# The first attention of a two-layer kernel: values stationary, the aggregate turned, norms from a product

## The chip, the cores and the metric

One Trainium2 chip (trn2), one core of it. The metric is the device time of one execution in microseconds (us), as the median of several runs. PE is TensorE (matrix products), DVE is VectorE, ACT is ScalarE, POOL is GpSimd, SP issues DMAs. All matrix products here are in float32 unless said otherwise; a float32 product shows as two MATMUL and two LDWEIGHTS records in the trace, a float32 transpose as one of each.

## The reference, cut to what matters

There are 4096 tokens in 16 sequences of 256, with 128 features. Four blocks follow each other: a recurrent mixer, a mixture of 32 small experts, the first attention, and a second attention with a mixture of 8 experts. The change touches the first attention alone:

```python
q, g = split(tokens @ Wqg)      # 16 heads, keys of 16, values and gates of 64
k, v = split(tokens @ Wkv)
q, k, v = l2norm(q), l2norm(k), l2norm(v)
attn = square(relu(q @ k.T))
aggr = attn @ v                 # per head: 256 x 64
n = norm(aggr, axis=-1)
out = tanh(n) * aggr / max(n, 1e-12) * tanh(silu(g))
y = out.reshape(tokens, 16 * 64) @ Wout
```

## The kernel before

The program has phases, one for each block; the first attention is the third, between two points at which all engines meet. Its work is one sequence at a time (256 queries and keys, in two tiles of 128), as a pipeline of four stages over the sequences: `fetch` (gather the expert outputs, form the input and normalise it), `front` (queries, keys, values, gates and their norms), `att` (scores, relu, square, aggregate) and `tail` (the last two aggregates, norms, gate, output product). `pipeline` calls each engine's `half(fetch, front, att, tail)` once for each step, with the sequences that stand one behind the other in the four stages; 19 steps in all, of which ten run in a loop of two steps a turn. Inside a step every engine goes through g = 0 to 7, the eight pairs of heads, and its program is written out by hand: what stands ahead of what on an engine is the order of the lines of `half`, and engines meet at semaphores alone. So a waiting instruction holds up all that stands behind it on its engine.

For each pair g PE makes the scores with keys on partitions (`scores`, L1091), ACT applies relu into one of four `attn` buffers (L831), DVE squares it (L1571), but POOL does for pairs 2, 3 and 6 (L601), and two pairs later PE adds up the aggregate (`aggregate`, L1103). There the squared scores are the stationary operand (128 columns) and the values the moving one (64 columns), so the aggregate has queries on partitions:

```python
mm = pe.matmul(psum[:, 4 + j, ...], attn[g % RING][:, h, ...128 queries], v[q.p][:, c, ...64], ...)
```

The aggregate of four pairs (half hf = 0 or 1) fills banks 4 and 5. Then the half's tail begins: ACT copies it out and squares it (`take_aggregate`, L843), DVE sums the squares over each head's 64 values (`norm_of`, L1573), POOL makes 1/length and length (`length_of`, L603: a power of -0.5, L608), ACT takes the tanh (L850), POOL scales the gate by tanh and 1/length (`scale_gate`, L612), DVE multiplies aggregate and gate (`gated_output`, L1578), PE turns the result (`turn_oT`, L1121), ACT and DVE copy one tile each out of PSUM (`take_oT`, L855 and L1583). When both halves are there, PE multiplies by Wout (L1168), DVE adds the residual (L1693) and SP stores it. The half 0 is worked on from g = 5 of stage `att` on, half 1 in stage `tail`.

Two PSUM banks (6 and 7, `ring`) serve all other products of the phase in turn; `fill` (L1083) waits for the last reader of a bank before it is written again. On DVE the inverse roots of the norms of queries, keys and values (`inverse_root`, twelve small instructions, L1550 to L1561) stand at g = 3 and give POOL the factor by which it scales the values (L648). `normalise3` (L1607) makes the next sequence's normalised input with the factor `rstd3` of POOL (L655); PE turns it (L1184), ACT copies it out as x3T (L904), and the next step's products start from it.

## Time and profile before

| what | us |
|---|---|
| median of 3 runs | 2004.08 |
| lowest, highest | 1994.43, 2009.70 |
| span of the profiled execution | 2019.7 |
| of it, the phase of the first attention | about 385 to 1225 |

The profiled execution has no other time beside its span; the span is 15.6 us above the median of the three runs. Rows of the timeline have the start, the duration from the first start to the last end of a merged piece, engine, line, names, shapes and count; [..] at the end is the idle time of the engine ahead of the piece and what ended it. PEclk is the share of TensorE's 2.4 GHz that was granted: 1.00 or, at the lower of its two levels (1.2 GHz), 0.50.

### The profile page before, as it was taken

What the parts mean: (1) busy time and instruction counts of PE and PEld (TensorE: products, weight loads), DVE (VectorE), ACT (ScalarE), POOL (GpSimd) and SP (SyncE); (2) the same over time, 40 slices, a digit from 0 to 9 for tenths busy, and PEclk for the clock granted to TensorE, in tenths of its full rate; (3) what the DMA queues carried; (4) which work ended last, traced back from release to release, by engine and by line L of the source; (5) the groups of instructions that cost most, each with busy time, mean ns of one, the idle gap of its engine ahead of it and who ended that gap; (6) DMA issues with size and microseconds to landing.
All of it is one profiled execution on the core that took longest, in us unless ns stands there. A gap on an engine that the chain in (4) does not pass through costs nothing.

```text
span 2019.7 us, 28317 instructions
## 1 busy us (share of the span) xinstructions
PE 1449.9 (72%) x8634; PEld 933.4 (46%) x8635; DVE 1233.7 (61%) x2840; ACT 750.5 (37%) x1206; POOL 949.0 (47%) x1080
## 2 busy tenths in 40 slices
PE   3434326478787878778878872899989989984876
PEld 2222214146665656566666671334333333334765
DVE  6877841387876777778778742565746556553332
ACT  1101002144444444444444430445544454541221
POOL 2346476466665656566666442131312213124554
PEclk7555555578887878888888875777876687786777
DMA  4000006100000000000000003000000000001110
GB/s 123 22 24 14 12 7 127 43 5 7 8 8 1 6 6 6 6 6 6 6 6 9 3 3 94 6 9 17 14 10 8 16 8 16 5 11 37 43 42 12
DMA packets 73355, 40.91 MB, mean 20 GB/s; under 512 B 23811, under 2 KB 68716, under 8 KB 73284
## 3 DMA queue, kind: packets, MB, share of 16 engines
q1 hardware_dynamic: 50530, 24.02, 4.3%
q0 software_dynamic: 20384, 11.67, 2.9%
q10 hardware_dynamic: 2370, 4.35, 0.8%
q8 instruction: 36, 0.59, 0.1%
q14 instruction: 35, 0.29, 0.1%
HBM read 31.11 MB, written 23.87 MB: 27 GB/s over the span
## 4 chain that ended last, share of the span: by engine, by line
PE 45%; DVE 25%; issue 10%; POOL 8%; ACT 5%; another core or an unknown queue 3%; DMA 2%; ACTq 1%; POOLq 1%; SPq 0%; DVEq 0%
PE psum L1117 8%; PE psum L1221 6%; PE psum L1242 5%; PE psum L1168 4%; DVE o L1581 3%; PE psum L1251 3%; PE psum L1211 2%; PE psum L1154 2%; POOL yg L631 2%; POOL out L753 2%; PE psum L1126 2%; PE psum L1145 1%; PE psum L1283 1%; DVE rden L1433 1%
## 5 line engine op out<-in xcount | busy, mean ns | idle before, releaser
L1117 PE MATMUL psum<-v,attn 128*128 128x64 f32 x2048 | 293.2, 304 | 25.6 <-ACT aggr L846 17.1
L1117 PEld LDWEIGHTS psum<-v,attn 128*128 128x128 f32 x2048 | 277.2, 217 | 61.9 <-issue 45.7
L1741 DVE TENSOR_REDUCE terms<-psum 128x2 bf16<-128x512 f32 x256 | 170.2, 692 | 94.8 <-PE psum L1242 87.0
L683 POOL TENSOR_SCALAR veps<-meanvar 128x2 f32<-128x2 f32 x32 | 6.1, 192 | 423.4 <-DVE meanvar L1719 423.4
L921 ACT ACTIVATE prob<-psum 128x512 f32<-128x512 f32 x256 | 143.6, 597 | 100.8 <-PE psum L1211 98.6
L1221 PE MATMUL psum<-prob,v 128*32 128x256 f32 x1024 | 172.2, 466 | 0.8 <-ACT pvT L926 0.8
L631 POOL DMA_INDIRECT yg<-ye_dram,routel x128 | 142.1, 1110 | 59.8 <-issue 37.3
L560 POOL DMA_INDIRECT xe_dram<-rows_out,route x128 | 130.9, 1023 | 39.7 <-issue 39.4
L1242 PE MATMUL psum<-k_highT,q_highT 32*128 32x256 bf16 x512 | 127.7, 344 | 29.7 <-DVE terms L1741 27.0
L1126 PE MATMUL psum<-ident,o 128*128 128x128 f32 x256 | 50.1, 360 | 118.8 <-DVE silu_g L1675 82.1
L831 ACT ACTIVATE attn<-psum 128x1024 f32<-128x1024 f32 x128 | 130.1, 1017 | 14.0 <-PE psum L1100 11.2
L608 POOL TENSOR_TENSOR o_inv<-o_max,minus_half 128x16 f32<-128x16 f32 x32 | 100.2, 3133 | 2.7
L1126 PEld LDWEIGHTS psum<-ident,o 128*128 128x128 f32 x256 | 40.1, 187 | 132.5 <-DVE o L1581 57.6
L648 POOL TENSOR_TENSOR v<-v,inv 128x2048 f32<-128x2048 f32 x16 | 70.7, 4419 | 63.1 <-DVE inv L1561 63.1
L1571 DVE TENSOR_TENSOR attn<-attn 128x1024 f32<-128x1024 f32 x80 | 99.3, 1242 | 0.0
L1581 DVE TENSOR_TENSOR o<-aggr,gate 128x1024 f32<-128x1024 f32 x32 | 90.1, 2815 | 13.6 <-POOL gate L620 13.6
L601 POOL TENSOR_TENSOR attn<-attn 128x1024 f32<-128x1024 f32 x48 | 91.1, 1897 | 7.9 <-ACT attn L831 7.9
L606 POOL TENSOR_SCALAR o_max<-o_norm 128x16 f32<-128x16 f32 x32 | 11.2, 350 | 176.1 <-DVE o_norm L1576 174.4
L1221 PEld LDWEIGHTS psum<-prob,v 128*32 128x32 f32 x1024 | 58.6, 125 | 71.1 <-issue 44.3
L1168 PE MATMUL psum<-w_out,oT 128*128 128x128 f32 x512 | 88.5, 353 | 0.9 <-DVE oT L1585 0.9
L1211 PE MATMUL psum<-qT,kT 64*128 64x256 bf16 x512 | 87.8, 314 | 0.0
L1168 PEld LDWEIGHTS psum<-w_out,oT 128*128 128x128 f32 x512 | 87.0, 268 | 1.2 <-issue 1.2
(300 smaller groups left out, 3088.7 us busy)
## 6 DMA issues: line engine op xcount, KB each, us to landing
x4n_dram<-x4n SPq DMA_DIRECT2D x16, 256.0 KB, 2.2
w<-in_w POOLq DMA_DIRECT2D x48, 64.0 KB, 2.7
x_in<-in_x SPq DMA_DIRECT2D x8, 256.0 KB, 2.9
xe_dram<-zero_rows SPq DMA_DIRECT2D x8, 256.0 KB, 3.3
x_dram<-x1s SPq DMA_DIRECT2D x8, 256.0 KB
xe_dram<-rows_out,route POOLq DMA_INDIRECT x128
xe<-xe_dram SPq DMA_DIRECT2D x16, 128.0 KB
ye_dram<-ye SPq DMA_DIRECT2D x16, 128.0 KB, 2.2
```

The costliest lines, as they stand in the source:

```text
L560: pool.indirect_dma_start(xe_dram, bass.IndirectOffsetOnAxis(ap=where[:, j, K0 + k:K0 + k + 1], axis=0), rows_out[p][:, j, :], None, bound ...
L631: pool.indirect_dma_start(yg[fetch.p][:, j, k, :], None, ye_dram, bass.IndirectOffsetOnAxis(ap=where[:, j, K0 + k:K0 + k + 1], axis=0), bo ...
L831: act.activation(r[:], psum[:, 2 * (g % 2):2 * (g % 2) + 2, :], ACT.Relu).then_inc(s["relu_made"], 1)
L921: act.activation(prob[head % 4][:], bank[head % 3][:], ACT.Exp, scale=SCALE).then_inc(s["exp_made"], 1)
L1117: mm = pe.matmul(psum[:, 4 + j, (head % HALF) * DV:(head % HALF + 1) * DV], attn[g % RING][:, h, c * SEQ + j * P:c * SEQ + (j + 1) * P], v ...
L1126: mm = pe.transpose(b[:, c * P:(c + 1) * P], o[:, j, c * P:(c + 1) * P], ident[:])
L1168: mm = pe.matmul(b[:, j * D:(j + 1) * D], oT[:, j, c, :], w_out[:, c, :], start=(c == 0), stop=(c == PAIRS - 1))
L1211: mm = pe.matmul(bank[head % 3][:, c * SEQ:(c + 1) * SEQ], kT4[att.p][part, head // 2, c * P:(c + 1) * P], qT4[att.p][part, head // 2, :], ...
L1221: mm = pe.matmul(bank[3][part, t * SEQ:(t + 1) * SEQ], v4[q.p][:, c, head, :], prob[head % 4][:, c * SEQ:(c + 1) * SEQ], start=(c == 0), s ...
L1242: mm = pe.matmul(bank[4 + a2][:, b2 * SEQ:(b2 + 1) * SEQ], q_highT[part, 2 * jp + b2, j * P:(j + 1) * P], k_highT[part, :], start=True, st ...
L1581: dve.tensor_tensor(o[:], aggr[:], gate[q.p][:, :, 512 * hf:512 * hf + 512], ALU.mult).then_inc(s["o_made"], 1)
L1741: dve.tensor_reduce(terms4[:, 0, j, head:head + 2, 6, 0], bank[4 + a2].rearrange("q (b k) -> q b k", b=2), AX, ALU.max, negate=True).then_ ...
```

## The change

The aggregate product swaps its operands: the 64 value columns of a head are loaded as weights and 256 queries stream past, so that the aggregate has the 64 dimensions of a head on partitions, two heads above each other (the heads of a pair write partitions 0 to 63 and 64 to 127). There are four products of 256 columns for a pair where there were eight of 64. It is already turned, so `turn_oT` and both `take_oT` go. In exchange the gate, scaled by POOL as before, is turned on PE (`turn_gate`), and DVE multiplies it straight out of PSUM into `oT` (`gated_output`, two instructions of 128x512 for a half where there were one of 128x1024 and a copy of 128x512). The sum of squares over a head now runs over partitions: PE multiplies the squared aggregate, as weights, by a new constant of two columns, `head_of`, that selects the head (`sum_squares`, eight products for a half), and DVE copies the 16 norms out of PSUM (`norm_of`). `aggr` has two buffers. The places in the order change too, as the diff shows.

```diff
-        aggr = sb("aggr", [P, 2, 512])
-        aggr_sq = sb("aggr_sq", [P, 2, 512])
-        o = sb("o", [P, 2, 512])
+        aggr = two("aggr", [P, 4, SEQ])
+        aggr_sq = sb("aggr_sq", [P, 4, SEQ])
...
                 if att:
                     length_of(att, 0)
+                if att:
+                    square(att, POOL_PAIRS[2])
                 if fetch:
                     hold(s["var3"], fetch.n)
...
                     pool.tensor_tensor(rstd3[:], veps3[:], minus_half[:, 0:2], ALU.pow).then_inc(s["rstd3"], 1)
                 if att:
                     scale_gate(att, 0)
-                if att:
-                    square(att, POOL_PAIRS[2])
...
             def take_aggregate(q, hf):
-                wait(act, s["o_made"], 2 * (q.n - 1) + hf)
+                wait(act, s["oT_made"], 4 * (q.n - 2) + 2 * hf + 2)
                 act.wait_ge(s["attn_read"], PAIRS * (q.n - 1) + 4 * hf + 4)
-                act.activation(aggr[:], psum[:, 4:6, :], ACT.Copy).then_inc(s["aggr_out"], 1)
+                act.activation(aggr[hf][:].rearrange("q (b a) t -> q b (a t)", b=2), psum[:, 4:6, :], ACT.Copy).then_inc(s["aggr_out"], 1)
...
-                    if tail and g == 0:
-                        take_aggregate(tail, 1)
-                    if tail and g == 2:
+                    if tail and g == 3:
                         tanh_of_norm(tail, 1)
                     if front and g in (1, 2):
...
+                    if tail and g == 1:
+                        take_aggregate(tail, 1)
...
-                    if front and g == 5:
-                        gate_tanh(front, 1)
-                    if att and g == 6:
+                    if att and g == 7:
                         tanh_of_norm(att, 0)
...
+                    if front and g == 6:
+                        gate_tanh(front, 0)
+                        gate_tanh(front, 1)
...
-                for j in range(2):
+                at = 4 + g % 4 // 2
+                for c in range(2):
                     for h in range(2):
                         head = 2 * g + h
-                        for c in range(2):
-                            mm = pe.matmul(psum[:, 4 + j, (head % HALF) * DV:(head % HALF + 1) * DV], attn[g % RING][:, h, c * SEQ + j * P:c * SEQ + (j + 1) * P],
-                                           v[q.p][:, c, head * DV:(head + 1) * DV], start=(c == 0), stop=(c == 1))
+                        mm = pe.matmul(psum[DV * h:DV * h + DV, at, g % 2 * SEQ:(g % 2 + 1) * SEQ], v[q.p][:, c, head * DV:(head + 1) * DV],
+                                       attn[g % RING][:, h, c * SEQ:(c + 1) * SEQ], start=(c == 0), stop=(c == 1))
...
-            def turn_oT(q, hf):
+            def sum_squares(q, hf, x):
+
+                m = 2 * (q.n - 1) + hf + 1
+                b = fill(x, [(s["o_norm_made"], m)], [(s["aggr_sq_made"], m)])
                 for j in range(2):
-                    x = OT_BANK[hf][j]
-                    b = fill(x, [(s["oT_dve" if j else "oT_act"], 2 * (q.n - 1) + hf + 1)], [(s["o_made"], 2 * (q.n - 1) + hf + 1)])
+                    for a4 in range(4):
+                        at = HALF * j + 2 * a4
+                        mm = pe.matmul(b[:, at:at + 2], aggr_sq[:, a4, j * P:(j + 1) * P], head_of[:], start=True, stop=True)
+                mm.then_inc(s["norm_ps"], 1)
+
+            def turn_gate(q, hf):
+                for j in range(2):
+                    m = 4 * (q.n - 1) + 2 * hf + j + 1
+                    b = fill(OT_BANK[hf][j], [(s["oT_made"], m)], [(s["gated"], m)])
                     for c in range(4):
-                        mm = pe.transpose(b[:, c * P:(c + 1) * P], o[:, j, c * P:(c + 1) * P], ident[:])
-                    mm.then_inc(s["oT_ps"], 1)
+                        mm = pe.transpose(b[:, c * P:(c + 1) * P], gate[q.p][:, j, 512 * hf + c * P:512 * hf + (c + 1) * P], ident[:])
+                    mm.then_inc(s["gateT_ps"], 1)
...
                     if tail and g == 1:
-                        turn_oT(tail, 0)
+                        turn_gate(tail, 0)
+                    if tail and g == 2:
+                        sum_squares(tail, 1, 0)
                     if tail and g == 5:
-                        turn_oT(tail, 1)
+                        turn_gate(tail, 1)
...
+                    if att and g == 6:
+                        sum_squares(att, 0, 1)
                     if fetch and g == 7:
                         b = fill(0, [], [(s["xn3_made"], fetch.n)])
...
             def norm_of(q, hf):
                 wait(dve, s["o_len_made"], 2 * (q.n - 1) + hf)
-                dve.wait_ge(s["aggr_sq_made"], 2 * (q.n - 1) + hf + 1)
-                dve.tensor_reduce(o_norm[:], aggr_sq[:].rearrange("q j (h d) -> q (j h) d", d=DV), AX, ALU.add).then_inc(s["o_norm_made"], 1)
+                dve.wait_ge(s["norm_ps"], 2 * (q.n - 1) + hf + 1)
+                dve.tensor_copy(o_norm[:], ring[1 - hf][:, 0:2 * HALF]).then_inc(s["o_norm_made"], 1)
...
             def gated_output(q, hf):
-                wait(dve, s["oT_ps"], 4 * (q.n - 1) + 2 * hf)
-                dve.wait_ge(s["gated"], 4 * (q.n - 1) + 2 * hf + 2)
-                dve.tensor_tensor(o[:], aggr[:], gate[q.p][:, :, 512 * hf:512 * hf + 512], ALU.mult).then_inc(s["o_made"], 1)
...
+                wait(dve, s["y3_ps"], q.n - 1)
+                dve.wait_ge(s["aggr_out"], 2 * (q.n - 1) + hf + 1)
+                for j in range(2):
+                    dve.wait_ge(s["gateT_ps"], 4 * (q.n - 1) + 2 * hf + j + 1)
+                    dve.tensor_tensor(oT[:, j, 4 * hf:4 * hf + 4, :], ring[OT_BANK[hf][j]][:].rearrange("q (c t) -> q c t", c=4), aggr[hf][:, :, j * P:(j + 1) * P], ALU.mult).then_inc(s["oT_made"], 1)
...
                     if tail and g == 1:
+                        gated_output(tail, 0)
+                    if tail and g == 2:
                         norm_of(tail, 1)
-                    if tail and g == 1:
-                        take_oT(tail, 0)
...
-                    if tail and g == 4:
-                        gated_output(tail, 1)
...
                     if tail and g == 5:
-                        take_oT(tail, 1)
-                    if att and g == 5:
-                        norm_of(att, 0)
+                        gated_output(tail, 1)
...
+                    if att and g == 6:
+                        norm_of(att, 0)
                     if fetch and g == 6:
                         normalise3(fetch)
-                    if att and g == 7:
-                        gated_output(att, 0)
```

What is left out: the declaration and the DMA of `head_of` among the weights, the names of semaphores, and the removed `take_oT` on ACT and DVE.

The three places that matter for the prediction, as they stand in the built programs. First PE, the last part of a step (g = 6 and 7), before: w_out with oT is the output product, ident with terms turns queries and keys, qT with kT are scores, v with attn the aggregate, ident with xn turns the next sequence's input.

```order
L1168 MATMUL psum<-w_out,oT 128x128 [waits oT_dve,oT_act]
L1168 MATMUL psum<-w_out,oT 128x128 x15
L1179 MATMUL psum<-ident,terms 128x128 [waits terms_made,oT_dve]
...
L1179 MATMUL psum<-ident,terms 128x128 [waits x3_made]
...
L1100 MATMUL psum<-qT,kT 128x256 [waits relu_made]
...
L1117 MATMUL psum<-v,attn 128x64 [waits attn_made]
...
L1179 MATMUL psum<-ident,terms 128x128 [waits qkT_act]
...
L1179 MATMUL psum<-ident,terms 128x128 [waits qkT_dve]
...
L1184 MATMUL psum<-ident,xn 128x128 [waits xn3_made,qkT_act]
```

And PE after, same place:

```order
L1172 MATMUL psum<-w_out,oT 128x128 [waits oT_made]
L1172 MATMUL psum<-w_out,oT 128x128 x15
L1183 MATMUL psum<-ident,terms 128x128 [waits terms_made,oT_made]
...
L1183 MATMUL psum<-ident,terms 128x128 [waits x3_made]
...
L1120 MATMUL psum<-head_of,aggr_sq 128x2 [waits aggr_sq_made,qkT_dve]
L1120 MATMUL psum<-head_of,aggr_sq 128x2 x7
L1092 MATMUL psum<-qT,kT 128x256 [waits relu_made]
...
L1109 MATMUL psum<-attn,v 64x256 [waits attn_made]
...
L1183 MATMUL psum<-ident,terms 128x128 [waits qkT_act]
...
L1183 MATMUL psum<-ident,terms 128x128 [waits o_norm_made]
...
L1190 MATMUL psum<-ident,xn 128x128 [waits xn3_made,qkT_act]
```

Behind the first two turns of terms stands a new block, the products of `aggr_sq` with `head_of`, which wait for the DVE copy of kT; the last turn before x3T now waits for the norms.

Second POOL, from the scaling of the values (v with inv) to the end of a step, before:

```order
L648 TENSOR_TENSOR v<-v,inv 128x2048 [waits v_copied]
...
L606 TENSOR_SCALAR o_max<-o_norm 128x16 [waits o_norm_made]
L608 TENSOR_TENSOR o_inv<-o_max,minus_half 128x16 [waits pool_chain]
L610 TENSOR_TENSOR o_len<-o_norm,o_inv 128x16 [waits pool_chain]
...
L653 TENSOR_SCALAR veps<-meanvar 128x2 [waits var3]
L655 TENSOR_TENSOR rstd<-veps,minus_half 128x2 [waits pool_chain]
...
L616 TENSOR_TENSOR o_factor<-o_tanh,o_inv 128x16 [waits gate_made,o_tanh_made]
L620 TENSOR_TENSOR gate<-gate,o_factor 128x512 [waits o_factor_made]
L620 TENSOR_TENSOR gate<-gate,o_factor 128x512
...
L601 TENSOR_TENSOR attn<-attn 128x1024 [waits relu_made]
```

After:

```order
L648 TENSOR_TENSOR v<-v,inv 128x2048 [waits v_copied]
...
L606 TENSOR_SCALAR o_max<-o_norm 128x16 [waits o_norm_made]
L608 TENSOR_TENSOR o_inv<-o_max,minus_half 128x16 [waits pool_chain]
L610 TENSOR_TENSOR o_len<-o_norm,o_inv 128x16 [waits pool_chain]
...
L601 TENSOR_TENSOR attn<-attn 128x1024 [waits relu_made]
...
L655 TENSOR_SCALAR veps<-meanvar 128x2 [waits var3]
L657 TENSOR_TENSOR rstd<-veps,minus_half 128x2 [waits pool_chain]
...
L616 TENSOR_TENSOR o_factor<-o_tanh,o_inv 128x16 [waits gate_made,o_tanh_made]
L620 TENSOR_TENSOR gate<-gate,o_factor 128x512 [waits o_factor_made]
L620 TENSOR_TENSOR gate<-gate,o_factor 128x512
```

The square of pair 6 (attn from attn) has moved from the end to between the lengths and rstd; the lengths still wait for o_norm.

Third DVE, g = 4 to 6, before: silu_g is the gate, attn the square, terms the split of queries and keys, x from yg the combination of expert outputs, xn the normalised input.

```order
L1581 TENSOR_TENSOR o<-aggr,gate 128x1024 [waits gated]
...
L1675 SCALAR_TENSOR_TENSOR silu_g<-tanh_g,psum 128x512 [waits g_tanh,gate_made] x2
...
L1571 TENSOR_TENSOR attn<-attn 128x1024 [waits relu_made]
L1626 TENSOR_TENSOR terms<-qk,terms 128x64x16 [waits high_made]
...
L1585 COPY oT<-psum 128x512 [waits dve_chain,oT_ps]
L1576 TENSOR_REDUCE o_norm<-aggr_sq 128x16 [waits aggr_sq_made,o_len_made]
...
L1594 SCALAR_TENSOR_TENSOR x<-yg,routel,x1l 128x128 [waits yg_landed1]
...
L1571 TENSOR_TENSOR attn<-attn 128x1024 [waits relu_made]
...
L1693 TENSOR_TENSOR x<-x_kept,psum 128x256 [waits y3_ps,x3_stored0]
L1697 COPY kT<-psum 128x1024 [waits terms_ps]
L1610 TENSOR_SCALAR xn<-x,meanvar,rstd 128x128 [waits rstd3,var3]
L1611 TENSOR_SCALAR xn<-x,meanvar,rstd 128x128
```

After:

```order
L1677 SCALAR_TENSOR_TENSOR silu_g<-tanh_g,psum 128x512 [waits g_tanh,gate_made] x2
...
L1577 TENSOR_TENSOR attn<-attn 128x1024 [waits relu_made]
L1630 TENSOR_TENSOR terms<-qk,terms 128x64x16 [waits high_made]
...
L1589 TENSOR_TENSOR oT<-psum,aggr 128x512 [waits gateT_ps]
...
L1589 TENSOR_TENSOR oT<-psum,aggr 128x512 [waits gateT_ps]
...
L1598 SCALAR_TENSOR_TENSOR x<-yg,routel,x1l 128x128 [waits yg_landed1]
...
L1577 TENSOR_TENSOR attn<-attn 128x1024 [waits relu_made]
...
L1693 TENSOR_TENSOR x<-x_kept,psum 128x256 [waits y3_ps,x3_stored0]
L1697 COPY kT<-psum 128x1024 [waits terms_ps]
L1582 COPY o_norm<-psum 128x16 [waits norm_ps,o_len_made]
L1614 TENSOR_SCALAR xn<-x,meanvar,rstd 128x128 [waits rstd3,var3]
L1615 TENSOR_SCALAR xn<-x,meanvar,rstd 128x128
```

The product of aggregate and gate has gone from ahead of the gate's silu to behind the split; o_norm, before a sum ahead of the combination of expert outputs, is now a copy that stands behind the first kT and directly ahead of xn.

## Rows read from the trace of the kernel before

**Rows 1.** The page: its first line
```profile
span 2019.7 us, 28317 instructions
```

**Rows 2.** Windows by stage: the columns, the first phases, the first attention
```profile
core 0: us, PE busy (x) PEld busy (x) DVE busy (x) ACT busy (x) POOL busy (x), PEclk, DMA share, GB/s
0.00:385.00 385.00, 144.07 (x608) 93.83 (x609) 225.67 (x666) 48.41 (x125) 191.98 (x239) 0.56 0.21 48
385.00:1225.00 840.00, 664.66 (x4192) 504.96 (x4192) 614.67 (x982) 390.56 (x512) 507.95 (x408) 0.82 0.03 6
```

**Rows 3.** Timeline of DVE: the sum x3 of sequence 1, then of 14
```profile
501.49 0.42 DVE L1693 TENSOR_TENSOR x<-x_kept,psum 128x256 f32<-128x256 f32 x1 [2.55 <-PE psum L1168]
...
1157.72 0.42 DVE L1693 TENSOR_TENSOR x<-x_kept,psum 128x256 f32<-128x256 f32 x1 [5.15 <-PE psum L1168]
```

**Rows 4.** Timeline of PE, one sequence: start, duration, idle time before
```profile
748.04 1.97 PE L1126 MATMUL psum<-ident,o 128*128 128x128 f32 x8 [4.94 <-DVE silu_g L1675]
...
751.78 3.67 PE L1117 MATMUL psum<-v,attn 128*128 128x64 f32 x16 [1.23 <-ACT aggr L846]
755.24 5.72 PE L1168 MATMUL psum<-w_out,oT 128*128 128x128 f32 x32
760.80 1.37 PE L1179 MATMUL psum<-ident,terms 128*128 128x128 f16 x16
...
766.06 0.43 PE L1184 MATMUL psum<-ident,xn 128*128 128x128 f32 x2 [0.74 <-ACT qT L900]
...
772.91 1.94 PE L1154 MATMUL psum<-w_v,x3T 128*128 128x512 f32 x4
776.03 1.09 PE L1126 MATMUL psum<-ident,o 128*128 128x128 f32 x8 [1.19 <-issue]
```

**Rows 5.** Timeline of DVE, same sequence
```profile
742.68 4.64 DVE L1581 TENSOR_TENSOR o<-aggr,gate 128x1024 f32<-128x1024 f32 x1
...
748.43 1.21 DVE L1571 TENSOR_TENSOR attn<-attn 128x1024 f32<-128x1024 f32 x1
749.57 1.21 DVE L1626 TENSOR_TENSOR terms<-qk,terms 128x1024 f16<-128x1024 f32 x1
...
776.02 1.21 DVE L1576 TENSOR_REDUCE o_norm<-aggr_sq 128x16 f32<-128x1024 f32 x1
...
785.14 1.46 DVE L1675 SCALAR_TENSOR_TENSOR silu_g<-tanh_g,psum 128x512 f32<-128x512 f32 x2 [1.17 <-ACT tanh_g L880]
786.52 0.69 DVE L1550 TENSOR_SCALAR norm<-norm 128x96 f32<-128x96 f32 x1
...
791.50 4.64 DVE L1581 TENSOR_TENSOR o<-aggr,gate 128x1024 f32<-128x1024 f32 x1
```

**Rows 6.** Timeline of POOL, same sequence
```profile
758.90 0.69 POOL L655 TENSOR_TENSOR rstd<-veps,minus_half 128x2 f32<-128x2 f32 x1
...
777.77 2.94 POOL L608 TENSOR_TENSOR o_inv<-o_max,minus_half 128x16 f32<-128x16 f32 x1
...
785.25 1.89 POOL L601 TENSOR_TENSOR attn<-attn 128x1024 f32<-128x1024 f32 x1
790.67 4.39 POOL L648 TENSOR_TENSOR v<-v,inv 128x2048 f32<-128x2048 f32 x1 [3.53 <-DVE inv L1561]
```

**Rows 7.** Timeline of ACT: the turned input x3T leaves PSUM
```profile
766.53 0.39 ACT L904 ACTIVATE x3T<-psum 128x256 f32<-128x256 f32 x1 [0.60 <-PE psum L1184]
```

**Rows 8.** Timeline of PE in the first phase: products of 64 weight columns
```profile
51.21 1.98 PE L1034 MATMUL psum<-x2T,sw 128*64 128x256 f32 x8
53.11 1.92 PE L1030 MATMUL psum<-gate_w,x2T 128*128 128x32 f32 x8
```

**Rows 9.** Windows: after PE's idle time, and later (columns as in rows 2)
```profile
748.00:759.00 11.00, 9.72 (x46) 8.93 (x47) 9.75 (x21) 5.59 (x7) 4.41 (x5) 0.50 0.00 0
759.00:791.00 32.00, 29.64 (x216) 21.30 (x215) 22.59 (x39) 17.92 (x24) 23.35 (x22) 1.00 0.04 9
```

**Rows 10.** Waits, 450 to 1150 us: what POOL waited for longest
```profile
POOL o_max L606 <- DVE o_norm L1576: 134.7, 21, 13.7
```

More of the change, by code:

```diff
@@ L194, in build_program @@
         head_mask = sb("head_mask", [P, 4])
+        head_of = sb("head_of", [P, 2])
         token_start = sb("token_start", [P, 2])
@@ L443, in _ @@
                              (b_o[:], a["b_o"].partition_broadcast(P)), (gate1_w[:], a["gate1_w"]),
-                             (gate1_b[:], a["gate1_b"].partition_broadcast(P)), (norms[:], a["norms"]), (head_mask[:], a["head_mask"]),
+                             (gate1_b[:], a["gate1_b"].partition_broadcast(P)), (norms[:], a["norms"]), (head_mask[:], a["head_mask"]), (head_of[:], a["head_of"]),
                              (token_start[:], a["token_start"]), (steps_of[:], a["steps_of"].partition_broadcast(P)),
@@ L838, in gate_tanh @@
             def gate_tanh(front, j):
-                wait(act, s["o_made"], 2 * (front.n - 2))
+                wait(act, s["gateT_ps"], 4 * (front.n - 2))
                 act.wait_ge(s["silu_made"], 4 * (front.n - 1) + 2 * j + 2)
@@ L1134, in half @@
                 elif tail:
-                    readers[0] = readers[1] = []
+                    readers[0], readers[1] = [], [(s["o_norm_made"], 2 * tail.n - 1)]
                 if front:
@@ L1660, in half @@
                     if tail and g == 1:
+                        gated_output(tail, 0)
+                    if tail and g == 2:
                         norm_of(tail, 1)
-                    if tail and g == 1:
-                        take_oT(tail, 0)
                     if front and g == 3:
@@ L1951, in lay_out @@
         "head_mask": (np.arange(P)[:, None] // DH % 4 == np.arange(4)[None, :]).astype(np.float32),
+        "head_of": (np.arange(P)[:, None] // DV == np.arange(2)[None, :]).astype(np.float32),
         "token_start": (np.arange(P)[:, None] + P * np.arange(2)[None, :]).astype(np.float32),
```

21 lines of the change are left out of this document (6 added, 15 removed).

## The prediction

> **What bounds the kernel now.** I read the page first, for the span [rows 1], then windows by stage. The first attention takes 840 us, and in them PE is busy 665, DVE 615, POOL 508 and ACT 391 [rows 2]: no engine is full, so the length comes from who waits for whom. The period next: the residual sum of sequence 1 starts at 501.49 and that of sequence 14 at 1157.72 [rows 3], so 13 steps take 656.2 us, 50.5 each. Some of them hold the turn of the loop and are longer; the step that I follow has none and takes 791.50 - 742.68 = 48.8 us from one product o to the next [rows 5]. Then the timelines, engine by engine, of that step. The reader is to see four things in them.
>
> 1. PE idles once for long: 4.94 us ahead of the turn at 748.04, until DVE has read a bank (silu_g) [rows 4]. DVE reads it late because o, ahead of it in its order, takes 4.64 us [rows 5].
> 2. o is slow because POOL scales the values meanwhile: 4.39 us at 790.67, and DVE's o at 791.50 ends (796.14) when POOL is through (795.06) and 1.2 us more have gone [rows 5, 6]. The small TENSOR_SCALAR at 786.52 takes 0.69 where it ends just behind POOL's square at 785.25; silu_g at 785.14, with one operand in PSUM, takes 1.46 for two beside the same square [rows 5, 6]. So a DVE instruction with all operands in SBUF can wait for POOL's to end, and one that reads PSUM does not.
> 3. Behind PE's long idle time the clock is down: 0.50 in 748 to 759, then 1.00 until 791 [rows 9]. The aggregate of a pair takes 3.67 at the lower clock [rows 4].
> 4. POOL waits 134.7 us in 21 times for o_norm [rows 10]; the norms of half 0 are still early enough: POOL has rstd by 758.90 + 0.69 = 759.6, while PE turns the next input only at 766.06 [rows 4, 6]. 6.5 us of slack, which the change spends.
>
> **What gets cheaper.** The aggregate of a pair: eight MATMUL records with 64 weight columns and 256 moving ones. The first phase has just that shape: x8 start at 51.21, and the next piece at 53.11, so 1.90 us, in a stage whose granted clock is 0.56 on average, so mostly 1.2 GHz [rows 2, 8]. The old aggregate takes 3.67 less an overlap of 0.2 at the lower clock, 3.47 [rows 4]. So the new one is 0.55 of it at the lower clock; at the higher one half of 1.90, 0.95, against 1.8. Some 0.85 x 8 = 6.8 us of PE a sequence. DVE loses o (4.64 and 1.2), two sums of 1.21 (one at 776.02 [rows 5]) and two copies of oT (some 0.65 each), 9.5 us, and gets four products out of PSUM of 0.65 and two small copies, 3 us. ACT loses two copies.
>
> **What gets dearer.** `sum_squares`: 16 weight loads of 128 columns for a half. The nearest row is the old aggregate itself, also 16 loads of 128 columns: 3.5 us at 1.2 GHz and 1.8 at 2.4 [rows 4], twice a sequence. PE is left with 6.8 - 3.6 = 3.2 us less. One DMA more for head_of lies among the weights, beside the first phases: nothing.
>
> The Trainium skill (TensorEngine Tiling (Array Packing), Key Properties) says that a change of tiling mode drains the array, which speaks against products of 64 columns between those of 128. The change of shape between 51.21 and 53.11 shows no gap [rows 8], and the row prevails: 0 us.
>
> **The path.** What decides is where the norms are now made. The chain that closes on itself in each step, with the time from x3T being ready (ACT, 766.53 + 0.39 = 766.92 [rows 7]):
>
> Front, to the norms of half 1. Before they are there at 776.02 + 1.21 = 777.24 [rows 5], 10.3 us behind x3T. Now: scores 0.3, w_qk 1.9 (as w_v at 772.91 [rows 4]), two aggregates 1.9, scores 0.3, w_v 1.8, the wait for DVE's copy 1.1 (from 774.85 to 776.03 [rows 4]), turn 1.0, scores 0.3, the wait for ACT's copy 0.4 and one aggregate 1.0, w_v 1.8, such a wait again 1.1, sum_squares 1.8, copy 0.3: 15.0 us.
>
> Middle, to w_out. Unchanged in kind: POOL's lengths, square, gate, square, from 777.24 to 785.25 + 1.89 = 787.14, 9.9 us [rows 5, 6]. Of them the lengths are 3.5 (the power 2.94 and two small ones). ACT's tanh of the gate stands behind the tanh of these lengths, so silu_g comes 2.2 us behind the lengths, and the inverse roots behind it meet POOL's gate and square, which run without a gap. With all operands in SBUF they wait, as at 786.52 [rows 5], and end 3.5 us behind the square (787.14 to 790.67 [rows 6]). Then POOL scales the values, 4.4, and now DVE's square of pair 4 is what waits for it, plus its own 1.2. Split 2.1, two products 1.3. In all 9.9 + 3.5 + 4.4 + 1.2 + 2.1 + 1.3 = 22.4 us. The saved o is thus given back: the block falls on the next instruction with SBUF operands.
>
> The Trainium skill states the rule behind it (SBUF — State Buffer, Who interferes with whom): a DVE instruction with two SBUF inputs contends with a GpSimd instruction that reads SBUF, and the second one blocks. The rows agree (4.64 against 1.2); were it not so the chain would be the 3.4 us shorter by which the short case below is shorter.
>
> End, from w_out to x3T. Before 766.92 - 755.24 = 11.7 us [rows 4, 7], since the norms of half 0 were made beside w_out. Now they stand behind it on PE: w_out 5.5 (as at 755.24, where half of it runs at the lower clock), the turns of terms 0.9, DVE's copy of kT 0.7, sum_squares 1.8, copy 0.3, POOL's lengths 3.5, then the square of pair 6 1.9, which was moved ahead of rstd, rstd 1.0 [rows 6], and xn, turn and copy out 3.2. The two xn cost 0.35 each, but POOL goes on with its gate and blocks the second; bounds 2.5 and 3.9. In all 18.8. Meanwhile PE has only scores, an aggregate and two turns, 2.2 us, and idles for some 6.
>
> That idle time is longer than the 4.94 behind which the clock stood at 0.50 for 11 us [rows 4, 9], so the next front begins at 1.2 GHz: its first 8 us of work can cost 4 more. Part of it lies under waits for DVE; I take 2.0, with 0 and 4.2 as bounds.
>
> Sum: 15.0 + 2.0 + 22.4 + 18.8 = 58.2 us a step against 48.8, so 9.4 more. This holds for the 13 steps between sequence 1 and 14 [rows 3]. In the last two steps nothing is fetched: no x3T waits; there the cheaper aggregates, which ran at the lower clock, give back what POOL's chain costs, and the first step with `att` has the new end once: together 0. So 13 x 9.4 = 122 us. The profiled execution would go from 2019.7 to 2142; from the median of the runs, 2004.1, the same step gives 2126.
>
> **The bounds.** Short: PE at 2.4 GHz throughout (w_out 3.7), the inverse roots run through beside POOL's square (3.4 less), xn at 2.5: 15.0 + 19.0 + 16.3 = 50.3 us, 1.5 more a step, 2024 us. Long: the lower clock in the front (4.2) and again from w_out to the norms (7.4, 1.9, 0.7 and 3.6 where 5.5, 0.9, 0.7 and 1.8 stand), xn at 3.9: 19.2 + 22.4 + 24.2 = 65.8, 17.0 more, 2225 us.
>
> **Rivals.**
> A, the other sign: PE was the bound and the norms come in time. For it: PE's one long idle time hung on o, and without it 4.9 us of waiting and the slow stretch behind it (an aggregate at 3.5 for 1.8, w_out 1.8 dearer, a turn 0.9) would go, 9 us, and PE's 3.2. If the new end cost only its PE work, a step would be near 42 to 44 us: 13 x 5.5 = 70 less, 1934 us. It decides at w_out: the new end is at least 16.3 us long where 11.7 were, so w_out would have to start 4.6 us earlier than now (37.1 behind x3T), and the middle alone, with the norms of half 1 later by 4.7, forbids that. Chance 0.07.
> B, the short case: the chain as I say, but unblocked and at the higher clock; 50 to 54 us a step, 2020 to 2070. For it: DVE is relieved of 6.5 us. Against: the block needs no coincidence, POOL follows its own order. Chance 0.17.
> C, the long case, over 62 us a step: the gaps ahead of the aggregates of pairs 2, 3 and 4 (2 to 4 us each) keep the clock down in the middle too. Over 2175. Chance 0.14.
> D, the change does not do what it says: products of 64 columns stream no faster than those of 128, 1.8 us a pair. Then the front is 2.6 us longer, a step 61, 2160. The rows of the first phase speak against it [rows 8]. Chance 0.04.
>
> My forecast, 54 to 62 us a step, has 0.58. Its own range is 2072 to 2176, and 2040 to 2190 leaves out 2 in 10. A measurement here tells about 1% (20 us) from no change. Faster by more than that is A, 0.06; within it lie the rest of A and the bottom of B, 0.07; slower is the rest, 0.87.
>
> **What would show it.** Right: o_norm of half 0 is made 7 us or more behind the start of w_out; PE waits for xn 5 us or more in each step, at the turn of the next input; POOL's lengths of half 1 start 14 to 19 us behind x3T where it was 10.3; the square of pair 4 takes 2.5 us or more, and the first inverse root over 2; products out of PSUM 0.65 each; an aggregate 0.95 at the higher clock; granted clock of the phase below what it is now. Wrong, if the residual sums come less than 50 us apart, if x3T waits for ACT's qT instead of xn, or if the aggregates still take 1.8 us.

## The result and the profile after

| | before | after |
|---|---|---|
| median of 4 runs each, us | 1999.26 (1969.48 to 2009.70) | 2132.9 (2126.89 to 2139.55) |
| after over before | | 1.0734, 95% interval 1.0623 to 1.0845 |
| span of the profiled execution, us | 2019.7 | 2131.2 |

The changed kernel is 7.3% slower. A ratio leaves out disturbed executions and the medians don't: for the run all_moves below only 3 of the 17 executions of before count (1965.6 to 1984.0 us), which is why its median lies under that of before and its ratio above 1. The page of after, its first line:

```profile
span 2131.2 us, 27346 instructions
```

The windows view of the first attention's phase, about 960 us long now (columns as in [rows 2]):

```profile
385.00:1345.00 960.00, 670.54 (x3678) 388.66 (x3677) 574.45 (x978) 376.95 (x479) 493.82 (x407) 0.77 0.02 5
```

PE has 514 MATMUL records fewer than in [rows 2] and is busy 6 us longer: what the smaller work saves, the lower granted clock (0.77 for 0.82) takes back. DVE is relieved of 40 us. Both are idle for longer, so the time went into waits. The residual sums of sequences 1 and 14, on DVE:

```profile
503.06 0.42 DVE L1693 TENSOR_TENSOR x<-x_kept,psum 128x256 f32<-128x256 f32 x1 [2.16 <-PE psum L1172]
...
1270.72 0.42 DVE L1693 TENSOR_TENSOR x<-x_kept,psum 128x256 f32<-128x256 f32 x1 [5.86 <-PE psum L1172]
```

13 steps take 767.7 us, 59.05 each, where [rows 3] gave 50.48. 13 x 8.57 = 111.4 us, as much as the whole difference of the two spans (111.5). Where a step's time goes, by engine, first PE's timeline from one turn of the next input (L1190) to the next:

```profile
751.10 0.69 PE L1190 MATMUL psum<-ident,xn 128*128 128x128 f32 x2 [6.15 <-DVE xn L1615]
...
752.36 3.07 PE L1147 MATMUL psum<-w_qk,x3T 128*128 128x512 f32 x4
755.36 1.08 PE L1109 MATMUL psum<-attn,v 128*64 128x256 f32 x8
756.38 0.39 PE L1092 MATMUL psum<-qT,kT 64*128 64x256 f16 x4
...
766.73 2.20 PE L1120 MATMUL psum<-head_of,aggr_sq 128*128 128x2 f32 x16 [1.19 <-DVE v L1659]
...
769.40 1.97 PE L1109 MATMUL psum<-attn,v 128*64 128x256 f32 x8
...
784.04 1.96 PE L1128 MATMUL psum<-ident,gate 128*128 128x128 f32 x8 [3.79 <-DVE silu_g L1677]
...
791.62 5.69 PE L1172 MATMUL psum<-w_out,oT 128*128 128x128 f32 x32 [1.72 <-DVE oT L1589]
...
799.30 1.95 PE L1120 MATMUL psum<-head_of,aggr_sq 128*128 128x2 f32 x16 [0.78 <-DVE kT L1697]
...
809.73 0.69 PE L1190 MATMUL psum<-ident,xn 128*128 128x128 f32 x2 [5.27 <-DVE xn L1615]
```

PE now idles 5 to 6 us ahead of L1190, a wait that was not there, and still 3.8 us ahead of the turned gate. An aggregate takes 1.02 us from its start to the next product's at the higher clock (755.36 to 756.38) and 1.91 at the lower (769.40 to w_g at 771.31). ACT's timeline has the copy x3T from which I count a step:

```profile
751.83 0.38 ACT L896 ACTIVATE x3T<-psum 128x256 f32<-128x256 f32 x1 [3.95 <-PE psum L1190]
...
810.46 0.38 ACT L896 ACTIVATE x3T<-psum 128x256 f32<-128x256 f32 x1 [3.96 <-PE psum L1190]
```

DVE's timeline of the same step:

```profile
769.04 0.17 DVE L1582 COPY o_norm<-psum 128x16 f32<-128x16 f32 x1 [2.44 <-PE psum L1120]
...
777.36 1.82 DVE L1558 TENSOR_SCALAR guess<-norm 128x96 uint32<-128x96 uint32 x1
779.21 0.21 DVE L1560 TENSOR_SCALAR inv<-guess 128x96 uint32<-128x96 uint32 x1
...
784.43 3.45 DVE L1577 TENSOR_TENSOR attn<-attn 128x1024 f32<-128x1024 f32 x1
...
790.18 1.29 DVE L1589 TENSOR_TENSOR oT<-psum,aggr 128x512 f32<-128x512 f32 x2 [0.31 <-DVE terms L1634]
...
801.35 0.17 DVE L1582 COPY o_norm<-psum 128x16 f32<-128x16 f32 x1 [2.11 <-PE psum L1120]
808.30 0.34 DVE L1614 TENSOR_SCALAR xn<-x,meanvar,rstd 128x128 f32<-128x128 f32 x1 [6.77 <-POOL rstd L657]
```

and POOL's:

```profile
769.42 0.26 POOL L606 TENSOR_SCALAR o_max<-o_norm 128x16 f32<-128x16 f32 x1 [6.06 <-DVE o_norm L1582]
...
777.22 1.89 POOL L601 TENSOR_TENSOR attn<-attn 128x1024 f32<-128x1024 f32 x1
782.39 4.40 POOL L648 TENSOR_TENSOR v<-v,inv 128x2048 f32<-128x2048 f32 x1 [3.29 <-DVE inv L1567]
801.72 0.25 POOL L606 TENSOR_SCALAR o_max<-o_norm 128x16 f32<-128x16 f32 x1 [14.93 <-DVE o_norm L1582]
...
805.25 1.89 POOL L601 TENSOR_TENSOR attn<-attn 128x1024 f32<-128x1024 f32 x1
...
807.50 0.69 POOL L657 TENSOR_TENSOR rstd<-veps,minus_half 128x2 f32<-128x2 f32 x1
```

Read from 801.35 on: the norms of half 0 are copied 4 us behind the end of w_out; POOL waits 14.93 us for them and has the lengths 3.7 us after the copy, then needs 1.9 for the square that was moved ahead and 1.0 for rstd; only then DVE can normalise, and PE turn, the next input. The waits of 450 to 1250 add this up (POOL's was 134.7 in [rows 10]):

```profile
POOL o_max L606 <- DVE o_norm L1582: 295.0, 27, 18.1
...
DVE xn L1614 <- POOL rstd L657: 94.9, 14, 6.8
PE psum L1190 <- DVE xn L1615: 79.6, 14, 6.2
```

The granted clock in this step, by windows:

```profile
750.00:760.00 10.00, 8.59 (x34) 3.38 (x34) 7.37 (x10) 4.00 (x6) 8.31 (x8) 0.77 0.01 1
...
769.00:772.00 3.00, 3.00 (x13) 1.27 (x10) 1.36 (x3) 1.02 (x1) 2.50 (x2) 0.50 0.00 0
...
785.00:791.00 6.00, 3.52 (x17) 1.50 (x15) 5.66 (x7) 2.46 (x3) 1.79 (x1) 0.50 0.00 0
...
801.00:809.00 8.00, 3.46 (x31) 2.38 (x30) 0.88 (x3) 2.15 (x3) 6.77 (x8) 0.59 0.00 0
```

It is down behind each of PE's long waits: when w_qk starts (3.07 us, where w_v, of the same shape, takes 1.98 at 2.4 GHz), and from the turned gate into w_out. It also falls at 769, behind sum_squares of half 1, with no idle time of PE over 1.2 us since 752; w_g there takes 3.78 us for 1.98.

### The profile page after: what moved, and what is told of

It reads as the page before. It is cut to its first block, busy times and chain, and to the rows that moved or that the text cites. A ratio compares the mean times of both kernels' runs of the same rounds, so it can differ in the third digit from the quotient of the medians.

```text
span 2131.2 us, 27346 instructions
## 1 busy us (share of the span) xinstructions
PE 1448.7 (68%) x8122; PEld 815.6 (38%) x8123; DVE 1194.9 (56%) x2840; ACT 736.0 (35%) x1174; POOL 936.2 (44%) x1080
## 4 chain that ended last, share of the span: by engine, by line
PE 40%; DVE 30%; issue 12%; POOL 11%; ACT 3%; DMA 2%; another core or an unknown queue 1%; ACTq 1%; POOLq 1%; DVEq 0%; SPq 0%
PE psum L1227 6%; PE psum L1172 4%; PE psum L1248 4%; POOL o_inv L608 4%; PE psum L1120 3%; PE psum L1109 3%; DVE attn L1577 3%; PE psum L1257 3%; PE psum L1147 3%; PE psum L1217 2%; POOL out L753 2%; POOL got L744 2%; DVE silu_g L1677 2%; DVE v L1659 1%; PE psum L1289 1%
## 5 line engine op out<-in xcount | busy, mean ns | idle before, releaser
L1109 PE MATMUL psum<-attn,v 128*64 128x256 f32 x1024 | 169.9, 462 | 60.4 <-POOL attn L601 30.7
L631 POOL DMA_INDIRECT yg<-ye_dram,routel x128 | 146.7, 1146 | 41.4 <-issue 37.0
L1577 DVE TENSOR_TENSOR attn<-attn 128x1024 f32<-128x1024 f32 x80 | 134.7, 1683 | 9.3 <-ACT attn L831 9.3
L1109 PEld LDWEIGHTS psum<-attn,v 128*64 128x64 f32 x1024 | 72.8, 158 | 136.4 <-issue 62.5
L1172 PE MATMUL psum<-w_out,oT 128*128 128x128 f32 x512 | 95.4, 372 | 23.7 <-DVE oT L1589 23.7
L1172 PEld LDWEIGHTS psum<-w_out,oT 128*128 128x128 f32 x512 | 92.6, 284 | 35.8 <-DVE oT L1589 35.4
L1128 PE MATMUL psum<-ident,gate 128*128 128x128 f32 x256 | 48.6, 351 | 70.7 <-DVE silu_g L1677 48.2
L608 POOL TENSOR_TENSOR o_inv<-o_max,minus_half 128x16 f32<-128x16 f32 x32 | 93.8, 2933 | 2.7
L1120 PE MATMUL psum<-head_of,aggr_sq 128*128 128x2 f32 x512 | 65.7, 259 | 33.0 <-DVE v L1659 16.4
L889 ACT ACTIVATE qT<-psum 128x1024 f16<-128x1024 f16 x32 | 32.5, 1016 | 158.2 <-PE psum L1183 158.1
L1227 PEld LDWEIGHTS psum<-prob,v 128*32 128x32 f32 x1024 | 58.2, 125 | 69.0 <-issue 39.8
```

Of the source, the lines that this page charges most:

```text
L608: n = chain.step(pool.tensor_tensor(o_inv[:], o_max[:], minus_half[:], ALU.pow))
L631: pool.indirect_dma_start(yg[fetch.p][:, j, k, :], None, ye_dram, bass.IndirectOffsetOnAxis(ap=where[:, j, K0 + k:K0 + k + 1], axis=0), bo ...
L1109: mm = pe.matmul(psum[DV * h:DV * h + DV, at, g % 2 * SEQ:(g % 2 + 1) * SEQ], v[q.p][:, c, head * DV:(head + 1) * DV], attn[g % RING][:, h ...
L1172: mm = pe.matmul(b[:, j * D:(j + 1) * D], oT[:, j, c, :], w_out[:, c, :], start=(c == 0), stop=(c == PAIRS - 1))
L1227: mm = pe.matmul(bank[3][part, t * SEQ:(t + 1) * SEQ], v4[q.p][:, c, head, :], prob[head % 4][:, c * SEQ:(c + 1) * SEQ], start=(c == 0), s ...
L1577: dve.tensor_tensor(r[:], r[:], r[:], ALU.mult).then_inc(s["attn_made"], 1)
```

## The experiments

**The theories.** The expectations name them so. T1: the chain of the prediction sets the step (front, POOL's lengths, the blocked square, w_out, norms of half 0, POOL, rstd, xn), and most of the loss is the place of the norms of half 0 and POOL's order behind them. T2, the rival: PE's own work at the lower clock sets it, and the waits only move about. All kernels but b_norm_late are edits of the changed one. "Step" is the mean of 13 as above, from one profiled execution of each kernel. Most medians are of 2 executions, those of the last three rows of 10 to 12; an empty bracket means the same before as in the row above.

| run | median us (before beside it) | ratio, 95% interval | step us |
|---|---|---|---|
| after | 2132.9 (1999.26) | 1.0734 (1.0623 to 1.0845) | 59.05 |
| rstd_first | 2107.94 (2007.89) | 1.0503 (1.0342 to 1.0664) | 56.99 |
| sq6_back | 2142.45 | 1.0675 (1.0514 to 1.0836) | 58.69 |
| norm_before_wout | 2056.22 | 1.0246 (1.0075 to 1.0416) | 54.34 |
| norm1_early | 2095.72 | 1.0442 (1.0280 to 1.0605) | 56.39 |
| b_norm_late | 2155.98 (2015.76) | 1.0721 (1.0600 to 1.0842) | 60.14 |
| small_v | 2079.81 | 1.0342 (1.0254 to 1.0430) | 55.93 |
| half_aggr | 2118.92 | 1.0537 (1.0439 to 1.0634) | 58.02 |
| rstd_tanh | 2052.36 (2004.55) | 1.0252 (1.0158 to 1.0346) | 52.85 |
| v_late | 2118.04 | 1.0580 (1.0484 to 1.0677) | 57.96 |
| both_norms | 2022.40 (2015.76) | 1.0020 (0.9962 to 1.0077) | 51.98 |
| all_moves | 1995.60 (2004.55) | 1.0068 (0.9996 to 1.0140) | 49.88 |
| norm_mid | 2000.31 (2004.47) | 1.0006 (0.9959 to 1.0052) | 50.73 |

**norm_before_wout**: the norms of half 0 ahead of w_out on PE and ahead of combine on DVE.

```diff
+                    if att and g == 6:
+                        sum_squares(att, 0, 1)
                     if tail and g == 6:
...
-                    if att and g == 6:
-                        sum_squares(att, 0, 1)
```

> The changed kernel with sum_squares of half 0 ahead of the output product on PE, and its copy on DVE ahead of the combination of expert outputs. Theory 1: w_out starts 2 to 3 us later, but POOL works beside it and x3T follows w_out by 13 us instead of 19; a step of 52 to 54, 2045 to 2075 us. Theory 2: PE's work is the same, 2133.

It went nearly so (54.3 us a step, the time inside the range): 4.7 us a step and half the loss, by order alone, with the same instructions.

**b_norm_late**, the other way round: the kernel before, with nothing but the norms of half 0 put where the change has them.

```diff
-                    if att and g == 5:
-                        norm_of(att, 0)
...
+                    if att and g == 6:
+                        norm_of(att, 0)
                     if fetch and g == 6:
                         normalise3(fetch)
```

> The kernel BEFORE with one line moved: DVE's sum for the norms of half 0 stands behind the first kT, directly ahead of xn, where the changed kernel has its copy. Nothing of the swap. Theory 1 (the place of the norms costs): the slack of 6.5 us is spent, x3T comes 4 us later, PE idles there for 4 us or more and starts the front at the lower clock; a step of 53 to 56 instead of 48.8, 2055 to 2095 us against 2000. Theory 2 (the swap and its products cost): as before, 2000.

Slower than expected by 60 us: this one move costs the old kernel as much as the whole change costs (1.0721 against 1.0734). A part of what I had left out stands in its timelines of PE and ACT:

```profile
884.64 1.89 PE L1179 MATMUL psum<-ident,terms 128*128 128x128 f16 x16 [4.63 <-ACT qT L900]
...
883.46 0.22 ACT L853 ACTIVATE o_tanh<-o_len 128x16 f32<-128x16 f32 x1 [12.34 <-POOL o_len L610]
883.58 1.00 ACT L900 ACTIVATE qT<-psum 128x1024 f16<-128x1024 f16 x1
```

ACT's tanh of the lengths waits 12.34 us, and ACT's copy qT, which frees a PSUM bank for PE, is queued behind it. The change moves the tanh from g = 6 to g = 7 and so avoids the worst of this. The other part is a wait in the front that the chain doesn't have. ACT's copy of the aggregate of half 1, first in before, then in this run:

```profile
616.43 1.02 ACT L846 ACTIVATE aggr<-psum 128x1024 f32<-128x1024 f32 x1 [6.82 <-remote]
...
835.71 1.02 ACT L846 ACTIVATE aggr<-psum 128x1024 f32<-128x1024 f32 x1 [4.97 <-remote]
```

The trace names no releaser, DVE stands still beside ACT, and both go on 2 to 4 us behind the end that the trace gives PE's aggregate. Before has this wait in three of its 13 steps, which are its three long ones, this run in nine, after in none; where it comes from is open. So the run shows that late norms cost without the swap too, but not how much of the 7% they are; for the changed kernel norm_before_wout tells that.

**norm1_early**: the norms of half 1 ahead of the value products of g = 2, on PE and on DVE.

> The changed kernel with sum_squares of half 1 ahead of the second pair of value products instead of behind it, and the copy on DVE likewise. Theory 1: the norms of half 1 come 13.4 us behind x3T instead of 17.0, and all of the middle with them; a step of 55, 2086 us. Theory 2: 2133.

The norms of half 1 come 13.8 and 15.0 us behind x3T, where in after they come 17.0 and 18.0, and the step loses 2.7 us: near what was expected. It is the other cost of where the norms stand.

**rstd_first**: POOL makes rstd ahead of the lengths and of the square of pair 6.

```diff
-                if att:
-                    length_of(att, 0)
-                if att:
-                    square(att, POOL_PAIRS[2])
                 if fetch:
                     hold(s["var3"], fetch.n)
...
+                if att:
+                    length_of(att, 0)
+                if att:
+                    square(att, POOL_PAIRS[2])
```

> The changed kernel with one thing moved: POOL makes rstd of the next sequence ahead of the lengths of half 0. Theory 1 (the step closes through the norms: sum_squares, POOL's lengths and square, rstd, xn, x3T): x3T comes some 6.5 us earlier, PE's wait of 5 to 6 us for xn falls under 1.5, and the clock holds in the front; a step of 50 to 52 us instead of 58.6, 2035 us in all (2020 to 2060). Theory 2 (the extra products of PE and their clock make it slower, the order on POOL does not matter): no change, 2133.

A miss: 57.0 for 50 to 52. POOL's rstd is early, as wanted, but x3T still comes 6.0 us behind the norms here, and up to 6.7 in other steps. Its timelines of PE and ACT:

```profile
858.48 0.43 PE L1190 MATMUL psum<-ident,xn 128*128 128x128 f32 x2 [1.65 <-ACT qT L889]
...
857.22 0.22 ACT L854 ACTIVATE o_tanh<-o_len 128x16 f32<-128x16 f32 x1 [2.74 <-POOL o_len L610]
857.34 1.01 ACT L889 ACTIVATE qT<-psum 128x1024 f16<-128x1024 f16 x1
```

PE waits no more for xn but for a bank that ACT's qT frees (1.65 us here, 3.3 in most steps), and qT is queued behind the tanh, which waits for POOL. So the same late norms reach PE over a second engine.

**rstd_tanh**: rstd_first, and ACT's tanh of half 0 behind its copy x3T.

> rstd_first with one more move: ACT's tanh of the lengths of half 0 stands behind the copies of qT and x3T instead of ahead of them. In rstd_first x3T came 6.0 us behind the norms of half 0 though rstd was long there; the theory is that qT waited behind that tanh, which waits for POOL's lengths. Then x3T comes 4.0 to 4.5 us behind the norms, PE's wait for qT goes from 1.65 us to under 0.8, a step 55.2 instead of 57.0, 2085 us. If another wait stood behind it (POOL's square ahead of DVE's, the clock), no change, 2108.

Better than expected by 33 us; the profile of PE and ACT shows both waits gone:

```profile
825.51 0.43 PE L1190 MATMUL psum<-ident,xn 128*128 128x128 f32 x2 [0.74 <-ACT qT L887]
...
826.51 1.96 PE L1147 MATMUL psum<-w_qk,x3T 128*128 128x512 f32 x4 [0.24 <-ACT x3T L894]
...
825.98 0.38 ACT L894 ACTIVATE x3T<-psum 128x256 f32<-128x256 f32 x1 [0.60 <-PE psum L1190]
```

x3T comes 3.7 and 4.6 us behind the norms in turn (9.3 in after), and a step is 6.2 us shorter than in after by two moves. PE has no long idle time there any more, and w_qk takes 1.96 instead of 3.07: the two waits had cost the clock too, which I had not counted and which explains about 1 us of the surplus.

**sq6_back**: POOL's square of pair 6 behind the gate again, where it stood before.

> The changed kernel with POOL's square of pair 6 back behind the scaling of the gate, as before the change. Theory 1: rstd is 1.9 us earlier, so is x3T; a step of 56.7, 2108 us. Theory 2: no change, 2133. A third way: the aggregate of pair 6 now waits for the square and takes the gain back, 2125 or more.

A miss: no gain. From the residual sum to the next x3T it is 1.9 us shorter (11.5 for 13.4), as the square is; but the norms of half 1 then come at 18.5 and 19.8 instead of 17.0 and 18.0. PE doesn't wait for POOL's square there (its first aggregate starts at 872.46, directly behind w_qk); w_qk runs at the lower clock throughout (3.76 us), and sum_squares waits 1.85 us for DVE's value copy, for 1.19 in after. What ties this to the place of the square is open. The move of the square is no net part of the loss.

**small_v**: POOL scales one of 64 value columns.

```diff
-                    pool.tensor_tensor(vv, vv, inv3[:, 4 * HEADS:].unsqueeze(2).to_broadcast([P, 2 * HEADS, DV]), ALU.mult).then_inc(s["v_made"], 1)
+                    pool.tensor_tensor(vv[:, :, 0:1], vv[:, :, 0:1], inv3[:, 4 * HEADS:].unsqueeze(2).to_broadcast([P, 2 * HEADS, 1]), ALU.mult).then_inc(s["v_made"], 1)
```

> The changed kernel with POOL's scaling of the values cut to one of 64 columns a head; the other 63 stay unscaled, which the output has then too. Theory 1: DVE's square of pair 4 no longer waits (1.2 us instead of 3.45), so w_out starts 2.2 us earlier; a step of 56.4, 2104 us. Rival (something else would hold w_out, such as PE's turn of the gate): under 10 us off, 2125 or more.

DVE's square of pair 4, which took 3.45 in after, runs through:

```profile
825.17 1.22 DVE L1577 TENSOR_TENSOR attn<-attn 128x1024 f32<-128x1024 f32 x1
```

The direction is T1's, the size is larger: 3.1 us a step for 2.2. w_out starts 1.6 and 2.2 us earlier; the rest lies behind it: in every second step w_out takes 3.81 us, all at 2.4 GHz, where in after it takes 5.7 or more.

**v_late**: POOL's scaling of the values waits for DVE's split into terms.

> The changed kernel where POOL scales the values only once DVE has split queries and keys; nothing is left out. If the block by this one POOL instruction costs what small_v gained, DVE's square of pair 4 falls to 1.2 us, the combination of expert outputs is blocked instead, beside w_out, and reaches into the residual sum by 1 us: a step of 57.0 to 57.8 instead of 58.6 to 59, 2105 to 2118 us. If the block only moves to the next thing on the chain: no change, 2133.

As expected, at the upper end. The scaling (3.62 us, from 844.89) no longer meets the square but the first combining products, whose operands are all in SBUF:

```profile
841.44 1.22 DVE L1578 TENSOR_TENSOR attn<-attn 128x1024 f32<-128x1024 f32 x1
...
846.16 2.77 DVE L1599 SCALAR_TENSOR_TENSOR x<-yg,routel,x1l 128x128 f32<-128x128 f32 x2
```

2.77 for 0.61 in after: the block of 2.2 us moved to an instruction that has time, beside w_out. 1.1 us a step.

**half_aggr**: the aggregate over the keys 0 to 127 alone, half of PE's aggregate work.

> The changed kernel with half of each aggregate left out (keys 128 to 255 are not added). PE loses 4 us of work a step at the higher clock, 7.6 at the lower. Theory 1: only the aggregates on the chain count (pairs 6, 7, 0 and 4: 0.5 to 0.9 each), 2.5 us a step, 2100 us. Theory 2 (PE's work sets the time): 5 to 6 us a step, 2060 us.

Half of the aggregates' records are worth 1.0 us a step, and PE's wait for xn grew from 79.6 to 88.5 us. Both expectations were too high, 2.5 us of T1 and 5 to 6 of T2. T2 falls: PE's work is not what sets the step, so making it cheaper, which is what the change does, could buy little.

**both_norms**: rstd_first, norm_before_wout and norm1_early.

> The changed kernel with three moves together: rstd first on POOL, sum_squares of half 0 ahead of the output product, and that of half 1 ahead of the second value products. Theory 1: front 13.4, middle 22.4, end 12 to 13 at the higher clock: a step of 48 to 50, 1990 to 2015 us, so about the kernel before. Theory 2: 2133.

The same time as before within 0.8%, by order alone, but 52.0 us a step for the 48 to 50 expected. The norms ahead of w_out now run at the lower clock, and PE still waits 1.92 us for qT. Its timelines of PE and ACT:

```profile
805.18 3.58 PE L1120 MATMUL psum<-head_of,aggr_sq 128*128 128x2 f32 x16 [1.01 <-DVE oT L1589]
...
820.13 0.43 PE L1190 MATMUL psum<-ident,xn 128*128 128x128 f32 x2 [1.92 <-ACT qT L889]
...
816.08 1.99 ACT L841 ACTIVATE gate<-silu_g 128x1024 f32<-128x1024 f32 x2
...
818.87 0.22 ACT L854 ACTIVATE o_tanh<-o_len 128x16 f32<-128x16 f32 x1
```

The tanh of the lengths waits for nothing here, since the early norms give POOL's lengths in time. PE has turned what qT copies by 818.22, and ACT comes to it at 818.98, from the two tanhs of the gate (1.99 us), which the change put there, and a relu: ACT's own work, some 0.8 of the 1.92 us. Moving the tanhs of the gate behind x3T was not tried.

**all_moves**: both_norms, the tanh behind x3T, and v_late.

> Five moves together in the changed kernel: those of both_norms (52.0 a step), the tanh of half 0 behind x3T, and the scaling of the values behind the split. If the chain is what sets the time, the last two give 1 to 2 us each: a step of 48 to 50, 1965 to 1995 us, 1 to 2 per cent under the kernel before. If PE's work is by now the bound: as both_norms, 2010 to 2020.

At the top of what was expected: about the time of before, and 9.2 us a step under after. The single gains (6.2, 4.7, 2.7, 1.1: 14.7 us) don't add up, since the first two take away the same wait of PE for xn: with early norms the tanh no longer waits, and with it moved PE still waits 1.81 us for qT. Something else stands in its way too. DVE copies the norms of half 1 3.1 us behind the end of sum_squares in 8 of the 13 steps, and the trace names no releaser; PE's clock falls in the same stretch, with PE busy 2.76 of the 3 us before it. The row and the windows:

```profile
814.42 0.17 DVE L1583 COPY o_norm<-psum 128x16 f32<-128x16 f32 x1 [4.59 <-remote]
```

```profile
808.00:811.00 3.00, 2.76 (x27) 2.11 (x23) 1.83 (x3) 2.21 (x3) 2.09 (x3) 1.00 0.02 3
811.00:814.00 3.00, 1.83 (x6) 0.47 (x5) 0.00 (x0) 0.00 (x0) 2.00 (x2) 0.61 0.02 1
```

**norm_mid**: all_moves, with that copy behind DVE's first value copy of g = 2.

> all_moves, with DVE's copy of the norms of half 1 moved from ahead of the first value copy of g = 2 to behind it (PE's order is that of all_moves). In all_moves this copy comes 3.1 us behind the end of sum_squares in every second step (811.34 to 814.42, the other step 1.4 us) with no releaser in the trace (35.3 us in 8 times), and DVE's two value copies and PE's second pair of w_v products stand behind it. Theory: the time goes with what the copy itself waits for; then the first value copy is made at once, the idle time stays ahead of the norms' copy, PE's second pair of w_v is as late as before, and the step stays at 49 to 50.5 us, 1985 to 2005. Rival 1: it goes with the place in DVE's program; then it stands ahead of the value copy now, at the same length, and the time is the same. Rival 2: it comes from how the copy meets the running products and goes when the copy is later; then the long step loses 3 us, the mean step is 48 to 48.5, 1965 to 1980, and this version beats both kernels by 1 to 2%.

The idle time did not stay with the norms. It now stands ahead of the value copy, with about the same length:

```profile
770.63 0.69 DVE L1662 COPY v<-psum 128x512 f32<-128x512 f32 x1 [3.97 <-PE psum L1159]
771.24 0.17 DVE L1583 COPY o_norm<-psum 128x16 f32<-128x16 f32 x1
```

So it goes with the place and not with the norms' semaphores, as rival 1 had it, and the time is the same (the profiled execution is the slowest of its twelve, 2019.5 us, so 50.7 a step is rather long). The value copy comes 1.4 us behind the end that the trace gives its products, which fits PE really being slower there than its records say; whether that, or DVE's side, causes it stays open. No version beats the kernel before by more than a measurement tells.

## Why the prediction was right

The forecast was slower, 2126 us, and 2132.9 came out. The chain held; with x3T there at 752.21 in the step shown:

- *Front, 15.0 + 2.0.* The norms of half 1 are copied at 769.21: 17.0; some steps have 18.0. That the 2.0 for the clock fit is half luck: w_qk accounts for 1.1 of them (3.0 to the next product for 1.9), and the rest is too low a price elsewhere, 2.3 us from sum_squares to its copy for 1.8, 3.2 for each w_v with its wait for 2.9.
- *Middle, 22.4.* From 769.21 to 791.62: 22.4. Its parts too: POOL's last square ends at 779.11, 9.9 on; the value scaling starts 3.3 behind it, where the prediction has 3.5; it takes 4.40; DVE's square of pair 4 ends 1.1 behind it, and w_out starts 3.7 later, for 3.4. Here the saved o was given back, as [rows 5, 6] let one see; small_v and v_late show that this block is real and worth 1 to 3 us a step.
- *End, 18.8.* From 791.62 to 810.84: 19.2. w_out and the turns up to sum_squares 7.7 for 7.1, sum_squares with its copy 2.2 for 2.1, lengths 3.7 for 3.5, square and rstd 2.9 for 2.9, and 2.65 for the 3.2 of xn, turn and copy.
- *The sum, 58.2.* 58.6 in that step, 59.05 on the mean. But the loss was reckoned against one step of 48.8, and before's mean is 50.48. The prediction put the difference down to the turn of the loop. That comes in every second step, while three of the 13 steps take 54 to 56 us, and these are the ones with the wait that b_norm_late showed, 6.82 us of ACT at 616.43; after has none of it, which the prediction did not foresee. So 8.6 a step came, not 9.4, and 111.5 us between the two profiled executions, not 122. The measured ratio, 1.073, is on the other side of the predicted 2126 / 2004 = 1.061; before's profiled execution was itself 20 us over its median, so single executions don't settle a difference of this size, and that 2126 lies so near 2132.9 is in part luck.
- *Nothing in the last steps.* The last two take 38.5 and 31.4 us for 39.9 and 27.2: 2.8 more, small but not 0.
- *Prices.* Aggregate 1.02 at the higher clock (0.95 foretold) and 1.91 at the lower (1.90); sum_squares 1.95 (1.8); two products out of PSUM 1.29 (1.3).
- *Signs.* All that it named came but one: no single inverse root takes over 2 us; the longest, at 777.36, takes 1.82.

Of the rivals, A (faster, PE is the bound) is refuted by the sign and by half_aggr; B and C by the step; D by the aggregate of 1.02. The two bounds of the step, 50.3 and 65.8, were wide for this; of what the short one needs, unblocked roots came in no version of the changed kernel, and a w_out at 2.4 GHz only in every second step of small_v.

The Trainium skill (SBUF — State Buffer, Who interferes with whom) has the rule by which DVE's square and POOL's scaling block each other, and small_v agrees: 1.22 us without it, 3.45 with it. The drain at a change of tiling mode that the Trainium skill names (TensorEngine Tiling (Array Packing), Key Properties) doesn't show in these rows: aggregates of 64 columns stand between products of 128 at 755.36 to 756.38 with no gap.

What the prediction did not see, and the runs did: the late norms reach PE by two ways, POOL's rstd and ACT's tanh ahead of qT. In after xn is ready at 809.68 and qT at 806.50, so mending the first way alone (rstd_first) can bring x3T only some 3 us forward and gave 2.1 us a step, and mending both gave 6.2. That also made my expectation for rstd_first too good and the one for b_norm_late too small.
